# q and k stacked by way of DRAM, and probabilities turned by transposing transfers instead of by TensorE

## The chip, the cores and the metric

The kernel runs on one core of a Trainium2 chip. The metric is device time in microseconds, the median of several executions. The five engines (TensorE or PE, VectorE or DVE, ScalarE or ACT, GpSimd or POOL, and SyncE or SP, which here only issues DMA transfers) run their own streams of instructions and meet on semaphores.

## The reference

64 graphs of 128 nodes with 384 features pass two pre-norm residual blocks, an attention with 12 heads and a graph network of two layers:

```
h = relu(layernorm(x))
q, k, v = h Wq^T, h Wk^T, h Wv^T + bv            # 12 heads of 32
scores = q k^T / sqrt(384) + 2 adj                # per head
p = softmax(scores); rows whose scores are all 0 give 0
x = x + (p v) Wo^T + bo
h = relu(layernorm(x))
for l in 0, 1:
    u_left, u_right = h (h Wl^T)^T, h (h Wr^T)^T  # / sqrt(384)
    u = u_left on and above the diagonal of adj, u_right below it (adj transposed)
    e = exp(u) * adj;  h = relu(norm((e / sum(e)) (h W_lin^T + b)) * a + b)
x = x + h
```

Inputs and output are 32-bit. The kernel keeps that precision by splitting each matmul operand into a high and a low part and adding three products (hi hi, hi lo, lo hi).

## The kernel before, in words

Two graphs (256 token rows) form a group; there are 32 groups. All weights are loaded once, split into high and low part, and stay in SBUF. Each group passes through a list of steps, and each engine has its own written-out list (the table ORDER), in which every step comes with an offset in groups: an engine goes through its list once for each group, and runs step s for group g + offset. So attention of group g + 1 interleaves with the first graph layer of group g and the second layer of group g - 1. Nothing is scheduled at run time; an engine stops at the first step whose semaphores are not there yet, and all behind it on that engine waits too. The table BANK gives each job of TensorE one of the eight PSUM banks; a job must wait until the one before it in its bank was read out (`wait_bank`).

The steps by name, with the digit j for the graph (0 or 1) and c for a third of the heads (four heads, 512 columns):

- T1a, T1b: transposes of the normed input (xn1); QK0 to QK2: q and k for all heads, six blocks of 128 features by 256 tokens, two a job; V0, V1: v.
- q3, k3 on SP (`stack`, line 294): transfers that stack high and low parts of q and k along the partitions (3 x 32), so that one matmul of a depth of 96 forms all three products of a head. Each reads 32 partitions of qk, and each of the two steps has 12.
- Sjc on TensorE: the scores of four heads; on VectorE Sjc: adds 2 adj, writes prob and takes the row's minimum; xjc on ScalarE: the exponential.
- Pjc: TensorE turns the four squares of probabilities (line 417, with the identity), ScalarE evicts the high part into pT (line 482), VectorE the low part (line 599). PVj: 36 matmuls of pT against v. pT has room for one graph, so a graph's Pjc wait for the PV of the graph before.
- OTj, WOj: attention output, transposed and projected. T2a, T2b: the second norm, transposed. N0k, HL0j, U0, C0j: first graph layer; HTa, HTb, N1k, HL1j, U1, C1j: second one. AT: adj transposed.

TensorE does the 24 transposes of a group in four places: four behind N02, eight behind C11, four ahead of PV0 and eight behind it.

## Time and profile before

| what | value |
|---|---|
| median of 3 runs | 1622.85 us (1622.07 to 1628.5) |
| the profiled execution | 1625.41 us, of which span 1623.7 us |
| PE busy | 1550.8 us (96%), 13888 matmuls |
| DVE busy | 1146.9 us (71%) |
| ACT busy | 922.7 us (57%) |
| POOL busy | 457.1 us (28%) |
| chain that ended last | PE 87%, SP's queue 7% |
| DMA | 76.19 MB, mean 47 GB/s |
| mean granted TensorE clock | 0.98 |

The span runs from the first to the last instruction of one profiled execution. Busy time counts an engine's instructions; matmuls overlap, so the distance between two starts in the timeline says more of a matmul's price than its length. The chain is followed back from the last instruction to what released each step. A group of rows names line, engine, operation, output and inputs, and shapes.

### The profile page before, as it was taken

Reading aid. Unit: us, or ns where it says so; the run is one execution under the profiler, and the core shown is the slowest. Engines: PE = TensorE matmul, PEld = TensorE weight load, DVE = VectorE, ACT = ScalarE, POOL = GpSimd, SP = SyncE. Lnnn points to the kernel's source line nnn. Section 1 sums busy time; section 2 is a strip of 40 time slices with the busy share of each in tenths; the row PEclk is TensorE's granted clock in tenths of the full one; section 3 lists DMA queues with packets and bytes.
Section 4 is the critical chain, followed back from the end, with each engine's and each line's share of the span. In section 5 each row is a group of like instructions: output and inputs, shape, how many; then the busy total and the mean of one; then the engine's idle time right before and its main releaser. Section 6 shows DMA issues by size and latency. Waiting matters only on the chain.

```text
span 1623.7 us, 39352 instructions
## 1 busy us (share of the span) xinstructions
PE 1550.8 (96%) x13888; PEld 1524.4 (94%) x13888; DVE 1146.9 (71%) x4303; ACT 922.7 (57%) x2155; POOL 457.1 (28%) x928
## 2 busy tenths in 40 slices
PE   3699999999999999999999999999999999999984
PEld 3699999999999999999999999999999999999974
DVE  5567777777777677776767777767777776777643
ACT  4456655566665566665556656555666655665632
POOL 4113222333232223322233323222332323332222
PEclk8789999999999999999999999999999999999996
DMA  6101112211112211112221111221111222111100
GB/s 212 40 21 41 43 50 54 53 44 31 47 44 50 54 50 30 42 44 50 53 54 43 33 45 44 50 53 50 33 40 42 53 50 53 46 30 46 31 11 20
DMA packets 116769, 76.19 MB, mean 47 GB/s; under 512 B 14282, under 2 KB 116432, under 8 KB 116576
## 3 DMA queue, kind: packets, MB, share of 16 engines
q1 hardware_dynamic: 116128, 73.06, 17.6%
q8 instruction: 115, 1.88, 0.5%
q14 instruction: 78, 0.64, 0.1%
q0 software_dynamic: 448, 0.60, 0.1%
HBM read 23.28 MB, written 12.58 MB: 22 GB/s over the span
## 4 chain that ended last, share of the span: by engine, by line
PE 87%; SPq 7%; DVE 2%; issue 1%; ACT 1%; DMA 1%; POOL 1%; DVEq 0%; ACTq 0%; POOLq 0%
PE bank L341 70%; SPq L297 6%; PE bank L417 5%; PE bank L347 4%; PE bank L410 3%; PE bank L401 3%; PE bank L423 1%; DMA k<-qk 1%; PE bank L435 0%; ACT prob L506 0%; DVE qk L599 0%; ACT qk L482 0%; SPq L304 0%; DMA x_sb<-x 0%; DVE weights L575 0%
## 5 line engine op out<-in xcount | busy, mean ns | idle before, releaser
L341 PE MATMUL bank<-h,weights 128*128 128x256 f32 x3456 | 429.9, 282 | 5.8 <-DVE h L740 5.1
L341 PEld LDWEIGHTS bank<-h,weights 128*128 128x128 f32 x3456 | 412.0, 190 | 6.7 <-issue 5.7
L506 ACT ACTIVATE prob<-prob,rmin 128x128 f32<-128x128 f32 x768 | 237.2, 404 | 49.9 <-DVE rmin L657 49.9
L341 PE MATMUL bank<-weights,h 128*128 128x384 f32 x1152 | 223.5, 338 | 0.0
L341 PE MATMUL bank<-hA,weights 128*128 128x256 f32 x1728 | 218.5, 283 | 1.4 <-DVE hA L599 1.4
L599 DVE TENSOR_TENSOR n<-bank,n 128x512 fp32r<-128x512 f32 x192 | 129.4, 687 | 122.8 <-ACT n L482 122.7
L341 PEld LDWEIGHTS bank<-hA,weights 128*128 128x128 f32 x1728 | 211.7, 190 | 1.7 <-DVE hA L599 1.7
L341 PEld LDWEIGHTS bank<-weights,h 128*128 128x128 f32 x1152 | 194.1, 188 | 0.0
L482 ACT ACTIVATE n<-bank 128x512 fp32r<-128x512 f32 x192 | 111.9, 606 | 113.9 <-PE bank L341 113.9
L657 DVE CUSTOM_DVE_ANT_0 prob<-bank,adj_sb 128x128 f32<-128x128 f32 x768 | 175.0, 287 | 0.2 <-issue 0.2
L482 ACT ACTIVATE qk<-bank 128x512 f16<-128x512 f32 x96 | 57.2, 595 | 170.5 <-PE bank L341 170.5
L341 PE MATMUL bank<-n,h 128*128 128x256 f32 x1152 | 153.4, 287 | 0.0
L599 DVE TENSOR_TENSOR pT<-bank,pT 128x512 f16<-128x512 f32 x192 | 125.2, 680 | 27.8 <-ACT pT L482 27.5
L341 PEld LDWEIGHTS bank<-n,h 128*128 128x128 f32 x1152 | 141.7, 191 | 0.2 <-issue 0.2
L800 POOL TENSOR_SCALAR less_mean_gnn<-mv_gnn 128x2 f32<-128x2 f32 x64 | 14.2, 222 | 426.8 <-DVE mv_gnn L604 426.8
L341 PE MATMUL bank<-weights,hA 128*128 128x384 f32 x576 | 115.3, 344 | 2.9 <-DVEq L589 2.9
L341 PE MATMUL bank<-weights,oT 128*128 128x384 f32 x576 | 115.4, 344 | 1.4 <-DVE oT L599 1.4
L482 ACT ACTIVATE pT<-bank 128x512 f16<-128x512 f32 x192 | 111.6, 625 | 2.1 <-PE bank L410 1.7
L417 PE MATMUL bank<-ident,prob 128*128 128x128 f32 x768 | 107.7, 277 | 3.9 <-ACT prob L506 3.9
L787 POOL TENSOR_SCALAR less_mean_ln<-mv_ln 128x2 f32<-128x2 f32 x64 | 14.2, 222 | 325.3 <-DVE mv_ln L604 325.3
L341 PEld LDWEIGHTS bank<-weights,hA 128*128 128x128 f32 x576 | 101.1, 190 | 3.1 <-issue 3.1
L341 PEld LDWEIGHTS bank<-weights,oT 128*128 128x128 f32 x576 | 99.0, 189 | 1.6 <-DVE oT L599 1.6
(107 smaller groups left out, 2652.2 us busy)
## 6 DMA issues: line engine op xcount, KB each, us to landing
q<-qk SPq DMA_DIRECT2D x384, 48.0 KB, 1.9
k<-qk SPq DMA_DIRECT2D x384, 48.0 KB, 2.0
x_sb<-x SPq DMA_DIRECT2D x32, 384.0 KB, 3.5
out<-x SPq DMA_DIRECT2D x32, 384.0 KB, 2.5
adj_sb<-adj SPq DMA_DIRECT2D x32, 128.0 KB, 2.1
prob<-w SPq DMA_DIRECT2D x4, 576.0 KB, 6.3
x<-w SPq DMA_DIRECT2D x3, 576.0 KB, 4.4
pT<-w SPq DMA_DIRECT2D x3, 576.0 KB, 5.4
```

What stands on the lines that cost most here:

```text
L297: sp.dma_start(dst[D * r:D * r + D, a:NH:HC, :], qk[D * a:D * a + D, part, first:first + C, :]).then_inc(s, 16)
L341: mm = pe.matmul(out, lhsT, rhs, start=(n == 0), stop=(n == len(pairs) - 1))
L347: mm = pe.transpose(bank(job)[:, n * T + j * P:n * T + (j + 1) * P], src[:, j, c * P:(c + 1) * P], ident[:, :])
L401: mm = pe.matmul(bank(step)[:, a * P:(a + 1) * P], q3[:, h, j * P:(j + 1) * P], k3[:, h, j * P:(j + 1) * P], start=True, stop=True)
L410: mm = pe.matmul(bank(step)[:, h * DA:(h + 1) * DA], pT[:, a, h, :], v2[:, b, j, h, :], start=(h == 0 and n == 0), stop=(n == 2), skip_gro ...
L417: mm = pe.transpose(bank(step)[:, a * P:(a + 1) * P], prob[:, j, c * HC + a, :], ident[:, :])
L423: mm = pe.transpose(bank(step)[:, c * P:(c + 1) * P], o_sb[:, j, c * P:(c + 1) * P], ident[:, :])
L482: act.activation(out, src, ACT.Copy).then_inc(s_hi, 1)
L506: e = act.activation(prob[:, j, h, :], prob[:, j, h, :], ACT.Exp, bias=rmin[:, j, h:h + 1], scale=-1.0)
L599: dve.tensor_tensor(out, src, hi_part if hi_part.dtype == F16 else hi_part.bitcast(F32), ALU.subtract).then_inc(free(job), 1)
L657: r = dve.tensor_tensor_reduce(prob[:, j, h, :], bank(step)[:, a * P:(a + 1) * P], adj_sb[:, p, j, :], -2.0, 3.0e38, ALU.add, ALU.min, rmi ...
L787: pool.tensor_scalar(less_mean[k][:, :], mv[k][:, :, 0], -1.0, None, ALU.mult)
```

## The change

Three things change.

First, q and k. Instead of 24 transfers from SBUF to SBUF, each QK job is stored to a scratch tensor in DRAM (qs0, qs1, qs2: 256 KB each), and q3 and k3 read it back in three loads each (192 KB, rows of 1536 B). The order of the heads inside q3 and k3 changes with that.

Second, the probabilities. TensorE turns nothing. ScalarE (ph) copies the exponentials to a 16-bit high part in SBUF, VectorE (pl) subtracts to form the low part, and SP turns each 128x512 piece of each part into pT with a transposing transfer (pth, ptl): twelve a group. PVj waits for the transfers' semaphores. prob now holds one graph and not two, so the scores Sjc of the next graph wait for the low part of the one before. The new tile pp holds both parts.

Third, all five tables of ORDER and the table BANK are rewritten; T1a, T1b and QK0 move to the end of the pass of the group before (offset 2), and U0's last steps to offset 0.

```diff
@@ ORDER (one line of each table; BANK and the rest are rewritten in the same way)
 "SP": [
-        ("out", -2), ("q3", 1), ("ld_x", 2), ("k3", 1), ("ld_adj", 2)],
+        ("out", -2), ("qs0", 1), ("ld_adj", 1), ("qs1", 1), ("qs2", 1), ("ld_x", 2), ("q3", 1), ("k3", 1), ("pth00", 1),
...
@@ -163,10 +165,13 @@
         hA = sb("hA", [P, 2, C, T], F32R)
         qk = sb("qk", [P, 2, 2 * C, T], F16)
         xn1 = qk[:, :, :, :].rearrange("p s c t -> p (s c t)").bitcast(F32).rearrange("p (g h) -> p g h", g=2 * G)[:, 0:G, :]
+
+        qk_dram = nc.dram_tensor("qk_parts", [2, P, 2, 2 * C, T], F16).ap()
         q3 = sb("q3", [3 * D, NH, T], F16)
         k3 = sb("k3", [3 * D, NH, T], F16)
         v2 = sb("v2", [P, 2, G, NH, DA], F16)
-        prob = sb("prob", [P, G, NH, P])
+        prob = sb("prob", [P, NH, P])
+        pp = sb("prob_parts", [P, 2, NH, P], F16)
         pT = sb("pT", [P, 2, NH, P], F16)
         o_sb = sb("o_sb", [P, G, H])
         oT = sb("oT", [P, 2, C, P], F32R)
@@ -212,7 +217,10 @@
         s_xn2 = [sem(f"xn2_{j}") for j in range(G)]
         s_xbo = [sem(f"x_plus_bo{j}") for j in range(G)]
         s_q3, s_k3 = sem("q3_in"), sem("k3_in")
+        s_qs = [sem(f"qk_out{k}") for k in range(3)]
         s_exp = [[sem(f"exps{j}{c}") for c in range(C)] for j in range(G)]
+        s_part = [[sem(f"prob_{n}{c}") for c in range(C)] for n in ("hi", "lo")]
+        s_turned = [[sem(f"prob_turned_{n}{c}") for c in range(C)] for n in ("hi", "lo")]
         s_stats = {k: sem(f"stats_{k}") for k in ("ln1", "ln2")}
         s_aggr = {k: sem(f"aggr_{k}") for k in ("ln1", "ln2")}
         s_row0 = [sem(f"row0_{j}") for j in range(G)]
@@ -237,14 +245,14 @@
         LOADS = ((0, 0), (1, 1), (2, 2), (3, 3), (4, 0), (5, 1), (6, 2), (7, 3), (8, 0), (9, 1))
         STAGE_OF = dict(LOADS)
         SPLIT_AFTER = {
-            "ACT": {"": (0,), "xn1_1": (1,), "T1b": (2, 3), "QK0": (4, 5), "QK1": (6,), "V1": (7,), "QK2": (8,), "V0": (9,)},
-            "DVE": {"ln1_ag": (0,), "T1b": (1, 2), "QK0": (3, 4), "QK1": (5,), "QK2": (6, 7), "V1": (8,), "V0": (9,)}}
+            "ACT": {"": (0,), "xn1_1": (1,), "T1a": (2, 3), "QK0": (4, 5), "QK1": (6,), "QK2": (7,), "V0": (8,), "V1": (9,)},
+            "DVE": {"ln1_ag": (0,), "T1a": (1, 2), "QK0": (3, 4), "QK1": (5,), "QK2": (6, 7), "V0": (8,), "V1": (9,)}}
 
         def staged(m):
-            prob_flat = prob[:, :, :, :].rearrange("p g h q -> p (g h q)")
             flat = (x1[:, :, :, :].rearrange("p k g h -> p (k g h)")[:, 0:C * H],
                     pT[:, :, :, :].rearrange("p s h q -> p (s h q)").bitcast(F32)[:, 0:C * H],
-                    prob_flat[:, 0:C * H], prob_flat[:, NH * P:NH * P + C * H])[STAGE_OF[m]]
+                    prob[:, :, :].rearrange("p h q -> p (h q)")[:, 0:C * H],
+                    pp[:, :, :, :].rearrange("p s h q -> p (s h q)").bitcast(F32)[:, 0:C * H])[STAGE_OF[m]]
             return flat.rearrange("p (c o) -> p c o", c=C)
 
         def wait_load(eng, m):
@@ -279,7 +287,7 @@
             eng.wait_ge(s_hi, hi_turn[job, g])
 
         PARTS = [(HI, HI), (HI, LO), (LO, HI)]
-        STACKED = 16 * 3 * HC
+        STACKED = 16 * 3
 
         block = ctx.enter_context(nc.Block())
 
@@ -291,10 +299,10 @@
                         sp.wait_ge(s_wlo, m - 3)
                     sp.dma_start(staged(m), w_d[m].rearrange("(c p) o -> p c o", p=P)).then_inc(s_wload[STAGE_OF[m]], 16)
 
-            def stack(dst, s, first, parts):
-                for a in range(HC):
-                    for r, part in enumerate(parts):
-                        sp.dma_start(dst[D * r:D * r + D, a:NH:HC, :], qk[D * a:D * a + D, part, first:first + C, :]).then_inc(s, 16)
+            def stack(dst, s, which, parts, p):
+                for r, part in enumerate(parts):
+                    heads = qk_dram[p, :, part, which * C:which * C + C, :].rearrange("(a d) c t -> d a (c t)", d=D)
+                    sp.dma_start(dst[D * r:D * r + D, :, :].rearrange("d (a c) t -> d a (c t)", a=HC), heads).then_inc(s, 16)
 
             def run(step, g):
                 p, n = g % 2, g // 2
@@ -309,17 +317,35 @@
                     wait_filled(sp, "AT", g - 2)
                     ge(sp, s_mask[1], g - 1)
                     sp.dma_start(adj_sb[:, p, :, :], adj_d[g * G:(g + 1) * G, :, :].rearrange("g p h -> p g h")).then_inc(s_adjin[p], 16)
+                elif step[:2] == "qs":
+                    k = int(step[2])
+                    ge(sp, s_q3, STACKED * (g - 1))
+                    ge(sp, s_k3, STACKED * (g - 1))
+                    wait_drained(sp, f"QK{k}", g)
+                    sp.dma_start(qk_dram[p, :, :, 2 * k:2 * k + 2, :], qk[:, :, 2 * k:2 * k + 2, :]).then_inc(s_qs[k], 16)
                 elif step in ("q3", "k3"):
                     for j in range(G):
                         for c in range(C):
                             wait_filled(sp, f"S{j}{c}", g - 1)
-                    wait_drained(sp, "QK1", g)
+                    sp.wait_ge(s_qs[1], 16 * (g + 1))
                     if step == "q3":
-                        wait_drained(sp, "QK0", g)
-                        stack(q3, s_q3, 0, (HI, LO, HI))
+                        sp.wait_ge(s_qs[0], 16 * (g + 1))
+                        stack(q3, s_q3, 0, (HI, LO, HI), p)
                     else:
-                        wait_drained(sp, "QK2", g)
-                        stack(k3, s_k3, C, (HI, HI, LO))
+                        sp.wait_ge(s_qs[2], 16 * (g + 1))
+                        stack(k3, s_k3, 1, (HI, HI, LO), p)
+                elif step[:2] == "pt":
+
+                    part, j, c = "hl".index(step[2]), int(step[3]), int(step[4])
+                    hs = slice(c * HC, (c + 1) * HC)
+                    if g == 0:
+                        sp.wait_ge(s_wlo, NW)
+                    sp.wait_ge(s_part[part][c], G * g + j + 1)
+                    if j == 0:
+                        wait_filled(sp, "PV1", g - 1)
+                    else:
+                        wait_filled(sp, "PV0", g)
+                    sp.dma_start_transpose(pT[:, part, hs, :], pp[:, part, hs, :].rearrange("p h q -> p (h q)")).then_inc(s_turned[part][c], 16)
                 elif step == "out":
                     for j in range(G):
                         sp.wait_ge(s_y[j], g + 1)
@@ -397,24 +423,18 @@
                     pe.wait_ge(s_q3, STACKED * (g + 1))
                     pe.wait_ge(s_k3, STACKED * (g + 1))
                     for a in range(HC):
-                        h = c * HC + a
-                        mm = pe.matmul(bank(step)[:, a * P:(a + 1) * P], q3[:, h, j * P:(j + 1) * P], k3[:, h, j * P:(j + 1) * P], start=True, stop=True)
+                        mm = pe.matmul(bank(step)[:, a * P:(a + 1) * P], q3[:, a * C + c, j * P:(j + 1) * P], k3[:, a * C + c, j * P:(j + 1) * P], start=True, stop=True)
                     mm.then_inc(full(step), 1)
                 elif step[:2] == "PV":
                     j = int(step[2])
                     wait_drained(pe, f"V{j}", g)
-                    for c in range(C):
-                        wait_drained(pe, f"P{j}{c}", g)
+                    for part in (HI, LO):
+                        for c in range(C):
+                            pe.wait_ge(s_turned[part][c], 16 * (G * g + j + 1))
                     for h in range(NH):
                         for n, (a, b) in enumerate(PARTS):
                             mm = pe.matmul(bank(step)[:, h * DA:(h + 1) * DA], pT[:, a, h, :], v2[:, b, j, h, :],
                                            start=(h == 0 and n == 0), stop=(n == 2), skip_group_check=True)
-                    mm.then_inc(full(step), 1)
-                elif step[0] == "P":
-                    j, c = int(step[1]), int(step[2])
-                    pe.wait_ge(s_exp[j][c], g + 1)
-                    for a in range(HC):
-                        mm = pe.transpose(bank(step)[:, a * P:(a + 1) * P], prob[:, j, c * HC + a, :], ident[:, :])
                     mm.then_inc(full(step), 1)
                 elif step[:2] == "OT":
                     j = int(step[2])
@@ -486,8 +506,8 @@
                 if step[:4] == "xn1_":
                     j = int(step[4])
                     act.wait_ge(s_ln["ln1"], g + 1)
-                    ge(act, s_q3, STACKED * g)
-                    ge(act, s_k3, STACKED * g)
+                    for k in range(3):
+                        ge(act, s_qs[k], 16 * g)
                     act.activation(xn1[:, j, :], x_sb[:, p, j, :], ACT.Relu, bias=shift["ln1"][:, j:j + 1], scale=scale["ln1"][:, j:j + 1]).then_inc(s_xn1[j], 1)
                 elif step == "T1a":
                     hi(step, g, hA[:, HI, 0:2, :], 2 * T, "p (c t) -> p c t", c=2)
@@ -503,15 +523,14 @@
                     j, c = int(step[1]), int(step[2])
                     wait_drained(act, f"S{j}{c}", g)
                     for h in range(c * HC, (c + 1) * HC):
-                        e = act.activation(prob[:, j, h, :], prob[:, j, h, :], ACT.Exp, bias=rmin[:, j, h:h + 1], scale=-1.0)
+                        e = act.activation(prob[:, h, :], prob[:, h, :], ACT.Exp, bias=rmin[:, j, h:h + 1], scale=-1.0)
                     e.then_inc(s_exp[j][c], 1)
-                elif step[0] == "P":
-                    j, c = int(step[1]), int(step[2])
-                    if j == 0:
-                        wait_filled(act, "PV1", g - 1)
-                    else:
-                        wait_filled(act, "PV0", g)
-                    hi(step, g, pT[:, HI, c * HC:(c + 1) * HC, :], HC * P, "p (h q) -> p h q", h=HC)
+                elif step[:2] == "ph":
+                    j, c = int(step[2]), int(step[3])
+                    hs = slice(c * HC, (c + 1) * HC)
+                    act.wait_ge(s_exp[j][c], g + 1)
+                    ge(act, s_turned[HI][c], 16 * (G * g + j))
+                    act.activation(pp[:, HI, hs, :], prob[:, hs, :], ACT.Copy).then_inc(s_part[HI][c], 1)
                 elif step[:2] == "OT":
                     j = int(step[2])
                     hi(step, g, oT[:, HI, :, :], H, "p (c q) -> p c q", c=C)
@@ -650,11 +669,12 @@
                     dve.wait_ge(s_adjin[p], 16 * (n + 1))
                     if g == 0:
                         dve.wait_ge(s_wlo, 8)
+                    ge(dve, s_part[LO][c], G * g + j)
                     wait_filled(dve, step, g)
                     take_wait(3 + j * C + c)
                     for a in range(HC):
                         h = c * HC + a
-                        r = dve.tensor_tensor_reduce(prob[:, j, h, :], bank(step)[:, a * P:(a + 1) * P], adj_sb[:, p, j, :],
+                        r = dve.tensor_tensor_reduce(prob[:, h, :], bank(step)[:, a * P:(a + 1) * P], adj_sb[:, p, j, :],
                                                      -2.0, 3.0e38, ALU.add, ALU.min, rmin[:, j, h:h + 1])
                     r.then_inc(free(step), 1)
                 elif step[0] == "r":
@@ -681,10 +701,12 @@
                         dve.scalar_tensor_tensor(out=o_sb[:, j, :].rearrange("p (h d) -> p h d", h=NH), in0=pv[:, :, 0:D], scalar=-1.0,
                                                  in1=rinv[:, j, :].unsqueeze(2).to_broadcast([P, NH, D]),
                                                  op0=ALU.mult, op1=ALU.mult).then_inc(free(job), 1)
-                elif step[0] == "P":
-                    j, c = int(step[1]), int(step[2])
+                elif step[:2] == "pl":
+                    j, c = int(step[2]), int(step[3])
                     hs = slice(c * HC, (c + 1) * HC)
-                    lo(step, g, pT[:, LO, hs, :], pT[:, HI, hs, :], HC * P, "p (h q) -> p h q", h=HC)
+                    dve.wait_ge(s_part[HI][c], G * g + j + 1)
+                    ge(dve, s_turned[LO][c], 16 * (G * g + j))
+                    dve.tensor_tensor(pp[:, LO, hs, :], prob[:, hs, :], pp[:, HI, hs, :], ALU.subtract).then_inc(s_part[LO][c], 1)
                 elif step[:2] == "OT":
                     lo(step, g, oT[:, LO, :, :], oT[:, HI, :, :], H, "p (c q) -> p c q", c=C)
                 elif step[:2] == "WO":

```

Where the steps land. First TensorE from PV0 (36 matmuls of v and pT) to PV1, before: the transposes of prob stand on both sides of PV0, PV1 comes before QK0 (18 matmuls of hA and weights).

```order
L417 MATMUL bank<-ident,prob 128x128 x4
L410 MATMUL bank<-v,pT 128x33 x36
L417 MATMUL bank<-ident,prob 128x128 x8
L435 MATMUL bank<-ident,adj_sb 128x128 x2
L341 MATMUL bank<-n,h 128x256 x18
L423 MATMUL bank<-ident,o_sb 128x128 x3
L341 MATMUL bank<-weights,h 128x384 x9
L341 MATMUL bank<-bias_rows,pick 128x384
L347 MATMUL bank<-ident,qk 128x128 x6
L410 MATMUL bank<-v,pT 128x33 x36
```

The same place afterwards; S10 (k, q) is just ahead of PV0.

```order
L426 MATMUL bank<-k,q 128x128 x4
L436 MATMUL bank<-v,pT 128x33 x36
L367 MATMUL bank<-n,h 128x256 x18
L373 MATMUL bank<-ident,qk 128x128 x6
L367 MATMUL bank<-weights,h 128x384 x9
L367 MATMUL bank<-bias_rows,pick 128x384
L443 MATMUL bank<-ident,o_sb 128x128 x3
L367 MATMUL bank<-hA,weights 128x256 x18
L367 MATMUL bank<-weights,oT 128x384 x9
L367 MATMUL bank<-hl,dT 128x386 x6
L436 MATMUL bank<-v,pT 128x33 x36
```

No transposes of prob are left. Between the two PV jobs stand U0, T1, HL01, OT0, QK0, WO0, C00 and C01; QK0, WO0 and the C jobs were behind PV1 before.

Second, SP's queue over one group, before: q3, the load of x, k3, the load of adj, the result.

```order
L297 DMA q<-qk 32x3x256 x12
L304 DMA x_sb<-x 128x2x384
L297 DMA k<-qk 32x3x256 x12
L311 DMA adj_sb<-adj 128x2x128
L326 DMA out<-x 128x2x384
```

Afterwards:

```order
L352 DMA out<-x 128x2x384
L325 DMA qk_parts<-qk 256x1x512
L319 DMA adj_sb<-adj 128x2x128
L325 DMA qk_parts<-qk 256x1x512 x2
L312 DMA x_sb<-x 128x2x384
L305 DMA q<-qk_parts 32x4x768 x3
L305 DMA k<-qk_parts 32x4x768 x3
L348 DMA_TRANSPOSE pT<-prob_parts 128x4x128 x12
```

The 24 small transfers became three stores and six loads, and twelve transposes stand behind them, ahead of the next group's result and stores.

Third, TensorE behind QK2 up to the first scores, afterwards (before, the scores stood behind all of N1, HL10, T2, U1 and HL11):

```order
L367 MATMUL bank<-hA,weights 128x256 x18
L367 MATMUL bank<-weights,oT 128x384 x9
L373 MATMUL bank<-ident,c_sb 128x128 x6
L367 MATMUL bank<-weights,hA 128x384 x9
L367 MATMUL bank<-bias_rows,pick 128x384
L367 MATMUL bank<-weights,hA 128x384 x9
L367 MATMUL bank<-bias_rows,pick 128x384
L367 MATMUL bank<-h,weights 128x256 x36
L426 MATMUL bank<-k,q 128x128 x4
```

The first scores now come behind WO1, HT, V0, V1 and two N1 jobs, and the other scores are spread over the pass in fours.

## Rows read from the trace of the kernel before

**Rows 1.** Busy time by stretch: stretch, its length, each engine, clock, DMA share, GB/s.

```profile
core 0: us, PE busy (x) PEld busy (x) DVE busy (x) ACT busy (x) POOL busy (x), PEclk, DMA share, GB/s
200.00:400.00 200.00, 199.88 (x1834) 197.30 (x1832) 148.86 (x560) 116.26 (x275) 56.97 (x117) 1.00 0.18 46
4.00:6.00 2.00, 0.00 (x0) 0.00 (x0) 1.26 (x5) 0.25 (x1) 0.36 (x2) 1.00 1.07 403
```

**Rows 2.** TensorE in order of time: start us, length us, engine, line, what.

```profile
803.39 0.83 PE L401 MATMUL bank<-k,q 96*128 96x128 f16 x12
...
808.81 0.60 PE L417 MATMUL bank<-ident,prob 128*128 128x128 f32 x4
809.17 0.77 PE L341 MATMUL bank<-hl,dT 128*128 128x386 f32 x3
...
810.60 1.03 PE L417 MATMUL bank<-ident,prob 128*128 128x128 f32 x8
811.39 2.30 PE L341 MATMUL bank<-h,weights 128*128 128x256 f32 x18
...
815.27 0.60 PE L417 MATMUL bank<-ident,prob 128*128 128x128 f32 x4
815.70 1.06 PE L410 MATMUL bank<-v,pT 128*128 128x33 f16 x36
816.61 1.07 PE L417 MATMUL bank<-ident,prob 128*128 128x128 f32 x8
817.52 0.38 PE L435 MATMUL bank<-ident,adj_sb 128*128 128x128 f32 x2
...
851.25 0.83 PE L401 MATMUL bank<-k,q 96*128 96x128 f16 x12
...
1522.09 0.84 PE L401 MATMUL bank<-k,q 96*128 96x128 f16 x12
```

**Rows 3.** Groups by line: shapes, count, busy us, mean ns, idle before.

```profile
L506 ACT ACTIVATE prob<-prob,rmin 128x128 f32<-128x128 f32 x768 | 237.2, 404 | 49.9 <-DVE rmin L657 49.9
...
L599 DVE TENSOR_TENSOR pT<-bank,pT 128x512 f16<-128x512 f32 x192 | 125.2, 680 | 27.8 <-ACT pT L482 27.5 <-issue 0.2
...
L482 ACT ACTIVATE pT<-bank 128x512 f16<-128x512 f32 x192 | 111.6, 625 | 2.1 <-PE bank L410 1.7
L417 PE MATMUL bank<-ident,prob 128*128 128x128 f32 x768 | 107.7, 277 | 3.9 <-ACT prob L506 3.9
```

**Rows 4.** The queue of SP in order of time, one stretch.

```profile
832.50 7.69 SPq L297 DMA_DIRECT2D q<-qk  x12
```

**Rows 5.** Transfers: what, count, KB each, median us to landing.

```profile
k<-qk SPq DMA_DIRECT2D x384, 48.0 KB, 2.0
x_sb<-x SPq DMA_DIRECT2D x32, 384.0 KB, 3.5
out<-x SPq DMA_DIRECT2D x32, 384.0 KB, 2.5
adj_sb<-adj SPq DMA_DIRECT2D x32, 128.0 KB, 2.1
prob<-w SPq DMA_DIRECT2D x4, 576.0 KB, 6.3
```

**Rows 6.** TensorE in order of time, from U0 to C00.

```profile
817.66 2.40 PE L341 MATMUL bank<-n,h 128*128 128x256 f32 x18
...
822.62 1.06 PE L410 MATMUL bank<-v,pT 128*128 128x33 f16 x36
823.53 1.83 PE L341 MATMUL bank<-weights,oT 128*128 128x384 f32 x9
...
828.38 0.49 PE L423 MATMUL bank<-ident,o_sb 128*128 128x128 f32 x3
```

**Rows 7.** TensorE in order of time, behind QK2.

```profile
832.95 1.75 PE L341 MATMUL bank<-weights,oT 128*128 128x384 f32 x9
...
838.70 6.28 PE L341 MATMUL bank<-h,weights 128*128 128x256 f32 x54
844.82 1.73 PE L341 MATMUL bank<-weights,h 128*128 128x384 f32 x9
```

24 lines of the change are left out of this document (12 added, 12 removed), and 40 rows, old and new, of the table ORDER.

## The prediction, on record before the changed kernel ran

> **What bounds the kernel now.** I read the busy shares by stretch first. Between 200 and 400 us TensorE is busy 199.9 of 200 us at a granted clock of 1.00, VectorE 148.9, ScalarE 116.3, and the DMA engines 18% [rows 1]. So TensorE sets the pace, and nothing is lost to waits there. The timeline of TensorE gives the pace itself: the twelve score matmuls of a group start at 803.39, those of the next at 851.25, and fifteen groups later than the first at 1522.09. That is 47.86 us for one group and (1522.09 - 803.39) / 15 = 47.91 us in the mean [rows 2]. 32 groups of 47.9 us are 1533 us; the remaining 91 us of the span of 1623.7 us are start and end, where the pipeline fills and drains. What takes time out of TensorE's row is worth its full length, as long as every input still arrives in time. What only shortens VectorE or ScalarE is worth nothing.
>
> **What the change removes from TensorE.** The 24 transposes of the probabilities of each group. Their grouped row says 107.7 us busy for 768, 277 ns each [rows 3], but matmuls overlap, so the distance between starts is the better measure: 808.81 to 809.17 is 0.36 us for four, 810.60 to 811.39 is 0.79 for eight, 815.27 to 815.70 is 0.43 for four, 816.61 to 817.52 is 0.91 for eight [rows 2]. Together 2.49 us a group, 79.7 us for 32 groups. The busy time of 107.7 us is the upper end, 79.7 the value I take; the lower end is nothing, if a new wait stands in the gap. All other matmuls stay in number and shape, so the new pace is 47.9 - 2.5 = 45.4 us if TensorE stays full.
>
> **ScalarE and VectorE.** Six evictions of 128x512 from PSUM on each (625 ns and 680 ns [rows 3]) become six copies or subtractions of the same 512 columns out of SBUF. Neither output nor element count changes; I take no difference. Even 0.1 us more for each of twelve would be hidden: VectorE would have 149/200 x 47.9 = 35.7 us of work in 45.4. The exponentials stay.
>
> **SP's queue.** Before, 24 small transfers stack q and k: twelve take 7.69 us, 0.64 us each [rows 4], about 15.4 us a group. Afterwards there are 3 stores to DRAM, 6 loads, and 12 transposes. The trace has no transpose, so its two costs are bounded: the time h that it holds the queue, and the time L from issue to landing. For h the lower end is 0.64 us [rows 4]; the upper end is its whole landing. For L the nearest rows are 48 KB in 2.0 us, the lower end, and 128 KB in 2.1; upper ends are 384 KB in 3.5 and 576 KB in 6.3 [rows 5]. I take h = 1.2 us, twice a plain issue, because the transfer must be cut into many blocks, and L = 2.9, which is the 2.1 of 128 KB with that extra hold and a little for the turning. Both are estimates. The queue then has 12 x 1.2 + 9 x 0.64 + three others at about 0.5 = 21.7 us of work in 45.4. It is not full; but it is in order, and all depends on where it must deliver.
>
> **Tightest place: PV1.** pT has room for one graph. The six transposes of graph 1 wait until PV0 has read it, and PV1 waits for all six. Between them TensorE now has U0, T1, HL01, OT0, QK0, WO0, C00 and C01. Before, the same work ran from 817.66 to 828.38 with PV1 in its midst (822.62 to 823.53): 10.72 - 0.91 = 9.81 us [rows 6], less 0.15 us for the tail of PV0's last matmul: 9.65 us of cover. Needed are five holds and one landing: 5 x 1.2 + 2.9 = 8.9 us. At the bounds the need is 5 x 0.64 + 2.0 = 5.2 us, which costs nothing, and 6 x 6.3 = 37.8, which costs 28 us a group. The last data is no later: ph10 stands behind the evictions of T1 on ScalarE. U0 is 18 matmuls of 256 columns, as an N job is (2.0 us [rows 7]), T1 six transposes at 0.1 us; then come two evictions (0.9), ph10 (0.6) and on VectorE pl10 (0.7) [rows 3]: about 4.9 us behind PV0, before the sixth transpose's turn at 6.0. So PV1 finds its data with about 0.7 us to spare. PV0's own six have over 20 us of matmuls behind S01; I cost them at nothing.
>
> **Second place: S00.** Scores of the next group now stand after N12 and N10, not after HL11. Behind QK2, TensorE has WO1, HT, V0, V1 (832.95 to 838.70, 5.75 us) and two of three N jobs (6.12 x 2/3 = 4.08) [rows 7]: 9.8 us. Needed: eviction 0.6 + 0.7 with handovers, 1.5 us; then SP issues qs2, ld_x and three q3 loads (5 x 0.6 = 3.0; qs2 lands meanwhile in 2.5, as the 384 KB store [rows 5]), two k3 issues (1.3), and the third lands after 3 us (between 2.0 and 3.5): 8.8 us. Bandwidth: 384 + 1152 KB at the 403 GB/s of the first weight loads [rows 1] is 3.9 us, and fits between. About 1 us to spare.
>
> **The sum.** The profiled execution took 1625.4 us (span 1623.7 and 1.7 around it), 2.6 us above the median of 1622.85. 1625.4 - 79.7 = 1545.7 us; against the median 1543.2. With two margins under 1 us and all tables rewritten I add 0.25 us a group for short stalls, 8 us: **1551 us**. Start and end stay: the first groups have fewer issues for q and k, but a longer way from exponential to PV0.
>
> **Two rules of the Trainium skill on the transposing transfer.** Rows first: a plain 128 KB transfer lands in 2.1 us [rows 5]. "Advanced Engine Details and Errata", X-Bar Transpose, says that on this chip such a transfer is as fast as a plain one; by that, L is 2.1 to 2.5 and the sum stays at 1543 to 1551. "VectorE: DVE Perf Modes", The three transpose paths, gives 1309 ns for one 128x128 square in 2-byte numbers, against 390 ns on TensorE; with four squares in series that would be 5.2 us a transfer, an estimate from that page alone, and far above 2000 us for the kernel. No run here shows either; the second speaks against the change and stands beside the third rival.
>
> **Rivals.**
> 1. *q and k come late* (S00 waits). If six loads into 32 partitions each run below the rate of the weight loads, or land in 4.5 us, the need becomes 10.3 to 11 us against 9.8: about 1.2 us a group, 38 us, 1589 us. For it: only 1 us to spare, and ld_x goes ahead of them. Against: DMA is busy 18% of the time.
> 2. *The transposes are a little slow.* With 5h + L between 9.65 and 12.1 us PV1 waits for a part of the gain; in the middle 1.2 us a group, 1589 us again, by 12.1 us all is lost.
> 3. *Slower: each transpose holds the queue until it has landed* (h = L). Place: SP between PV0 and PV1. It decides from 5h + L = 9.65 + 2.49 = 12.1 us, h about 2.0. At 2.1 us (128 KB) the need is 12.6, 0.5 us a group above break-even: 1623 + 32 x 0.5 = 1639. At 2.8, midway to the 384 KB load, it is 16.8: 4.7 us a group lost, 1773. At 3.5 it is 21 us, 1908. For it: a chain of six with one buffer pays any hold six times. Against: plain transfers leave the queue after 0.64 of 2.0 us. The square rule above would fall here.
> 4. *The gap does not become time.* The single probability buffer (S1c waits for the subtraction of S0c) or the new bank table stalls TensorE 2.5 us a group: no change, 1623. Against: between S02 and S12, and between S01 and S11, stand two larger jobs of TensorE each, about 4 us, and four exponentials (404 ns each, overlapped [rows 3]), copy and subtraction need about 3.
>
> **Chances.** Forecast 0.55 (own range 1538 to 1570), first rival 0.15, second 0.12, third 0.14, fourth 0.04. A measurement of this kernel can tell 0.5%, some 8 us, from no change. Faster: 0.55 + 0.15 + 0.12 = 0.82; within 0.5%: 0.04; slower: 0.14. Eight in ten: the low end is 1538, a gain a little over 79.7 us (the whole 107.7 would give 1515, which counts overlapped time twice); the high end, reaching into the mild part of the third rival, 1640.
>
> **What would show it.** Right: distance between groups about 45.5 us, TensorE without a wait from 100 us on, no row of the transposes of prob on it, its wait for pT and k3 near nothing; SP's timeline with transposes 1.2 us apart and landing under 3.6. Wrong: TensorE's PV matmuls waiting for the DMA into pT, with transposes over 1.4 us apart (second or third rival); score matmuls waiting for k (first); waits for VectorE on a bank (fourth); or a granted clock under 1.00 in mid-kernel, as in the first 100 us, which would follow from such waits and make them dearer.

## The result and the profile after

The changed kernel takes 1643.15 us in the median of four runs (1639.69 to 1653.48); the kernel before took 1624.3 beside it. The ratio is 1.012, with a 95% interval from 1.0075 to 1.0165: slower by more than 0.5%, where 1551 us was forecast. The profiled execution took 1639.69 us.

The page of the changed kernel: busy time by engine, the chain that ended last, and its transfers with KB each and us to landing.

```profile
PE 1495.5 (91%) x13120; PEld 1459.9 (89%) x13120; DVE 1207.0 (74%) x4303; ACT 921.3 (56%) x2155; POOL 483.2 (30%) x928
...
PE 73%; DMA 13%; SPq 7%; issue 3%; DVE 3%; ACT 1%; POOL 1%; DVEq 0%; POOLq 0%; ACTq 0%
...
qk_parts<-qk SPq DMA_DIRECT2D x96, 256.0 KB, 2.5
q<-qk_parts SPq DMA_DIRECT2D x96, 192.0 KB, 4.5
k<-qk_parts SPq DMA_DIRECT2D x96, 192.0 KB, 5.5
x_sb<-x SPq DMA_DIRECT2D x32, 384.0 KB, 4.1
out<-x SPq DMA_DIRECT2D x32, 384.0 KB, 2.7
pT<-prob_parts SPq DMA_TRANSPOSE x384, 2.5
```

TensorE lost exactly the 768 transposes (13888 matmuls before, 13120 now) and about 55 us of busy time, where the forecast took 79.7 out. But transfers, 1% of the chain before, are 13% of it now. The landings answer to [rows 5]: the three loads of 192 KB into k3 take 5.5 us in the median, longer than 384 KB of x, and the transposing transfer takes 2.5.

Busy time by stretch, the answer to [rows 1]; the columns are the same.

```profile
200.00:400.00 200.00, 190.97 (x1683) 186.79 (x1682) 155.04 (x549) 116.39 (x275) 61.89 (x115) 0.99 0.42 93
...
844.00:846.00 2.00, 2.00 (x16) 2.00 (x15) 1.33 (x7) 0.18 (x1) 0.44 (x2) 1.00 0.82 252
846.00:848.00 2.00, 2.00 (x20) 2.00 (x19) 1.37 (x6) 0.43 (x1) 0.92 (x3) 1.00 0.97 274
848.00:850.00 2.00, 1.66 (x15) 1.45 (x13) 1.41 (x3) 2.00 (x5) 1.34 (x4) 1.00 0.91 188
```

TensorE is now idle for 9 us of 200, where it was idle for 0.1. From 846 to 850 us the DMA engines are nearly full (shares 0.97 and 0.91) and move only 274 and 188 GB/s; the first weight loads moved 403 [rows 1].

TensorE's waits: what waited for what, us in total, times, longest. In the changed kernel L426 is the line of the score matmuls, L436 that of PV, and L367 a helper that issues most of the others. "issue" names no engine: the profile shows nothing that TensorE waited for.

```profile
PE bank L426 <- DMA k<-qk_parts: 62.1, 31, 6.7
PE bank L367 <- issue: 13.9, 30, 3.1
PE bank L436 <- DMA pT<-prob_parts: 12.6, 5, 10.4
PE bank L367 <- DVEq L608: 11.1, 1, 11.1
```

The first scores wait for k in nearly every group. PV waits for pT five times, 10.4 of 12.6 us at the start. In order of time, on TensorE and then on SP's queue:

```profile
829.13 2.29 PE L367 MATMUL bank<-hA,weights 128*128 128x256 f32 x18 [0.35 <-issue]
...
837.27 2.37 PE L367 MATMUL bank<-hA,weights 128*128 128x256 f32 x18
839.47 1.75 PE L367 MATMUL bank<-weights,oT 128*128 128x384 f32 x9
...
851.23 0.38 PE L426 MATMUL bank<-k,q 96*128 96x128 f16 x4 [1.58 <-DMA k<-qk_parts]
```

```profile
839.34 2.26 SPq L325 DMA_DIRECT2D qk_parts<-qk  x2
841.99 0.38 SPq L312 DMA_DIRECT2D x_sb<-x  x1
842.66 1.71 SPq L305 DMA_DIRECT2D q<-qk_parts  x3
844.66 1.25 SPq L305 DMA_DIRECT2D k<-qk_parts  x3
```

QK2 starts at 837.27 and the job behind it at 839.47. The third load of k3 is issued at about 845.5, lands 5.6 us later, and TensorE goes on at 851.23. The distance of the first scores of two groups answers to [rows 2]: group 2 stands at 128.72 and group 31 at 1523.20, that is 48.09 us a group. Before, the same two stand at 133.04 and 1522.09, 47.90 us. So the middle of the program has won nothing.

### The profile page after: what moved, and what is told of

It is laid out like the page before. It is cut to its first block, busy times and chain, and to the rows that moved or that the text cites. A ratio compares the mean times of both kernels' runs of the same rounds, so it can differ in the third digit from the quotient of the medians.

```text
span 1638.0 us, 38385 instructions
## 1 busy us (share of the span) xinstructions
PE 1495.5 (91%) x13120; PEld 1459.9 (89%) x13120; DVE 1207.0 (74%) x4303; ACT 921.3 (56%) x2155; POOL 483.2 (30%) x928
## 4 chain that ended last, share of the span: by engine, by line
PE 73%; DMA 13%; SPq 7%; issue 3%; DVE 3%; ACT 1%; POOL 1%; DVEq 0%; POOLq 0%; ACTq 0%
PE bank L367 62%; DMA k<-qk_parts 11%; SPq L305 4%; PE bank L436 4%; PE bank L426 3%; PE bank L373 3%; SPq L348 1%; PE bank L443 1%; DVE x L717 1%; SPq L312 1%; DMA pT<-prob_parts 1%; DMA qk_parts<-qk 1%; DMA pT<-w 0%; PE bank L455 0%; DMA x_sb<-x 0%
## 5 line engine op out<-in xcount | busy, mean ns | idle before, releaser
L367 PE MATMUL bank<-h,weights 128*128 128x256 f32 x3456 | 435.9, 284 | 5.7 <-DVE h L762 4.7
L367 PEld LDWEIGHTS bank<-h,weights 128*128 128x128 f32 x3456 | 418.1, 192 | 6.7 <-issue 6.7
L526 ACT ACTIVATE prob<-prob,rmin 128x128 f32<-128x128 f32 x768 | 244.3, 394 | 23.1 <-DVE rmin L677 22.9
L367 PE MATMUL bank<-hA,weights 128*128 128x256 f32 x1728 | 229.8, 287 | 11.8 <-issue 9.8
L367 PE MATMUL bank<-weights,h 128*128 128x384 f32 x1152 | 229.9, 344 | 0.0
L367 PEld LDWEIGHTS bank<-hA,weights 128*128 128x128 f32 x1728 | 212.9, 191 | 18.8 <-issue 16.8
L367 PEld LDWEIGHTS bank<-weights,h 128*128 128x128 f32 x1152 | 197.2, 190 | 0.0
L842 POOL TENSOR_TENSOR x_sb<-x_sb,bo_all 128x384 f32<-128x384 f32 x64 | 65.0, 1016 | 442.9 <-ACT qk L511 437.6
L709 DVE TENSOR_TENSOR prob_parts<-prob,prob_parts 128x512 f16<-128x512 f32 x192 | 151.9, 791 | 7.1 <-ACT prob_parts L533 6.9
L367 PE MATMUL bank<-n,h 128*128 128x256 f32 x1152 | 153.1, 287 | 0.3 <-DVE n L618 0.3
L367 PEld LDWEIGHTS bank<-n,h 128*128 128x128 f32 x1152 | 141.4, 191 | 0.7 <-issue 0.7
L502 ACT ACTIVATE oT<-bank 128x384 fp32r<-128x384 f32 x64 | 31.5, 492 | 192.7 <-PE bank L443 192.7
L426 PE MATMUL bank<-k,q 96*128 96x128 f16 x768 | 76.2, 225 | 62.1 <-DMA k<-qk_parts 62.1
L367 PE MATMUL bank<-weights,hA 128*128 128x384 f32 x576 | 117.2, 348 | 11.1 <-DVEq L608 11.1
L533 ACT ACTIVATE prob_parts<-prob 128x512 f16<-128x512 f32 x192 | 120.2, 626 | 2.7 <-DMA pT<-prob_parts 1.5
L426 PEld LDWEIGHTS bank<-k,q 96*128 96x128 f16 x768 | 50.9, 100 | 75.8 <-issue 72.6
L367 PE MATMUL bank<-weights,oT 128*128 128x384 f32 x576 | 114.6, 344 | 3.2 <-DVE oT L618 3.2
L367 PEld LDWEIGHTS bank<-weights,hA 128*128 128x128 f32 x576 | 103.1, 192 | 11.3 <-issue 11.3
```

What stands on the lines that cost most here:

```text
L367: mm = pe.matmul(out, lhsT, rhs, start=(n == 0), stop=(n == len(pairs) - 1))
L426: mm = pe.matmul(bank(step)[:, a * P:(a + 1) * P], q3[:, a * C + c, j * P:(j + 1) * P], k3[:, a * C + c, j * P:(j + 1) * P], start=True, s ...
L502: act.activation(out, src, ACT.Copy).then_inc(s_hi, 1)
L526: e = act.activation(prob[:, h, :], prob[:, h, :], ACT.Exp, bias=rmin[:, j, h:h + 1], scale=-1.0)
L533: act.activation(pp[:, HI, hs, :], prob[:, hs, :], ACT.Copy).then_inc(s_part[HI][c], 1)
L709: dve.tensor_tensor(pp[:, LO, hs, :], prob[:, hs, :], pp[:, HI, hs, :], ALU.subtract).then_inc(s_part[LO][c], 1)
```

## The experiments

Theory A: the 2.5 us a group that the transposes took are free now, and the wait for k, with what follows from it, eats them. Its rivals name other holders: the DRAM route as such, the latency of one load and not its bytes, the transposing transfers, slow VectorE operations. Distances below are means from group 2 to 31 unless said otherwise; medians are in us, with the ratio to the kernel before and its interval. Of the waits for k, 9 to 12 us stand in the first two groups in each version of the changed kernel in this table.

| kernel | median | ratio | wait of TensorE for k (times) | k lands in |
|---|---|---|---|---|
| changed kernel | 1643.15 | 1.012 (1.0075 to 1.0165) | 62.1 (31) | 5.5 |
| S00 behind N11 | 1588.44 | 0.9771 (0.9754 to 0.9789) | 13.3 (6) | 5.4 |
| third loads cut | 1601.92 | 0.9849 (0.9829 to 0.9869) | 28.2 (27) | 4.4, the cut one 4.6 |
| x behind k | 1600.25 | 0.985 (0.9836 to 0.9865) | 23.0 (21) | 4.5 |
| loads to 128 partitions | 1587.78 | 0.9768 (0.9751 to 0.9784) | 19.1 (17) | 3.7 |
| before, DRAM route alone | 1617.57 | 0.9944 (0.9927 to 0.9961) | 15.9 (2) | 5.4 |
| before, transposing transfers alone | 1706.8 | 1.0503 (1.0482 to 1.0525) | 71.5 (32) | 1.9 |

**The first scores one job later.**

```diff
 "PE":
-  ("N10", -1), ("S00", 1), ("N11", -1), ("T2b", 0), ...
+  ("N10", -1), ("N11", -1), ("S00", 1), ("T2b", 0), ...
 (on VectorE S00 goes behind N11 too)
```

> The changed kernel with one move: S00 stands behind N11 instead of ahead of it, on TensorE and VectorE (one N job, 2.05 us, more cover for the loads of q3 and k3). Theory A (the scores wait for k3 because 1.5 MB of loads move at only some 225 GB/s, a wait of 1.75 us in each of 30 groups, and it alone eats the gain): the wait for k all but goes, the distance between groups falls from 47.9 to about 46.0 us, the time from 1643 to 1580-1592 us. Theory B (the re-sequencing as a whole is too tight, and another wait takes the place): distance stays above 47.3 us, time 1625-1643 us, with a new wait for a bank or for pT on TensorE.

Measured: 1588.44 us. k still lands in 5.4 us, but TensorE now has one more job of about 2.1 us ahead of S00. 49 of the 62 us of waiting are gone, and 55 us of time. The distance of first scores is 46.44 us. From group 2 on, TensorE waits for k only four times, 2.0 us in all. Theory A holds: it was the place of this one step that made the changed kernel slower than the kernel before. The 37 us that are left above the forecast of 1551 it does not explain.

**The DRAM route alone, in the kernel before.**

```diff
 "SP": [
-  ("out", -2), ("q3", 1), ("ld_x", 2), ("k3", 1), ("ld_adj", 2)],
+  ("out", -2), ("qs0", 1), ("qs1", 1), ("qs2", 1), ("q3", 1), ("ld_x", 2), ("k3", 1), ("ld_adj", 2)],
```

> The kernel before with the q and k route alone: three stores to DRAM and six loads a group instead of 24 small transfers; order of all compute engines as before, TensorE still turns the probabilities. Theory A (the route is harmless where the first scores come late, since here they stand behind N11, HL10, T2, U1 and HL11, 8.5 us later): no wait for k in mid-kernel, distance 47.9 us, time within 0.5% of before, 1616-1630 us. Theory C (the way through DRAM costs time by itself, in contention or latency): over 1635 us with waits for k in the middle.

Measured: 1617.57 us, a little faster than before. k lands in 5.4 us here too, and apart from two waits at the start nobody waits for it: S00 stands behind HL11 in that order. The same slow load costs nothing in one order and 55 us in another. The small gain has its place too, the even pace: the kernel before waits for k in five groups of the middle, 2.3 us in all, and its first scores are 47.90 us apart; here they are 47.72 to 47.73 apart in every group.

**Bytes or latency.** The third load of each of q3 and k3 is cut to an eighth.

```diff
-  sp.dma_start(dst[D * r:D * r + D, :, :]..., heads)
+  n = C * T // 8 if r == 2 and g > 0 else C * T
+  sp.dma_start(dst[D * r:D * r + D, :, :]...[:, :, 0:n], heads[:, :, 0:n])
```

> The changed kernel; from the second group on the third load of q3 and of k3 brings only an eighth of its bytes (the rest of those rows stays from the first group, so the low-high product of the scores is left out in part). Issues, waits and order are the same; 344 KB less in each burst. Theory A (the wait is bytes over a rate of some 225 GB/s): k3 lands 1.5 us earlier, the wait falls from 1.75 to 0.2-0.4 us, time about 1590-1602 us. Theory D (the wait is latency of store, load and issue, whatever the bytes): landing of k3 stays over 5 us, time 1636-1645 us.

Measured: 1601.92 us. The full loads of k land in 4.4 us, and the third, with 24 KB, in 4.6; it stands behind the others in the queue. With as many loads and fewer bytes, the wait falls by more than half. A fixed latency would have left it.

**The place of x.** ld_x goes behind k3.

```diff
-  ("qs2", 1), ("ld_x", 2), ("q3", 1), ("k3", 1), ("pth00", 1),
+  ("qs2", 1), ("q3", 1), ("k3", 1), ("ld_x", 2), ("pth00", 1),
```

> The changed kernel with one transfer moved on SP: the load of x (384 KB) goes out behind the six loads of q3 and k3 instead of ahead of them, and the first norm's statistics stand later on VectorE to match; TensorE's order is untouched. If the bytes ahead of k3's last load at its rate decide when k lands (the theory), 384 KB less at some 225 GB/s is 1.7 us earlier, TensorE's wait for k (62.1 us) falls below 15 us, and 1590 to 1605 us come out, with x landing later and nobody waiting for it. Rival: only the bytes to 32 partitions count, which the load of x (128 partitions) does not share; then k lands less than 0.7 us earlier and the time stays above 1620 us.

Measured: 1600.25 us; k in 4.5 us, x in 5.3. k lands 1 us earlier, less than the 1.7 expected but more than the rival's 0.7. The wait left is 23.0 us, above the 15 expected. The short wait ahead of QK0, 0.35 us a group in the changed kernel, grows to about 0.5 and has a name here: 18.1 us in 30 times for the low part of hA on VectorE. Bytes to all partitions count too, as bytes ahead in the same queue.

**Where the loads go.** The same 192 KB in the same 1536 B rows, but to 128 partitions.

```diff
+  if g > 0:
+      rows = qk_dram[p, :, part, which * C:which * C + C, :].rearrange("p c t -> p (c t)")
+      sp.dma_start(dst[:, 4 * r:4 * r + 3, :].rearrange("p h t -> p (h t)"), rows)
```

> The changed kernel with its order untouched; from the second group on the six loads that fill q3 and k3 bring the same 192 KB each, in the same rows of 1536 B, but spread over 128 partitions instead of 32, so the scores are computed from wrongly placed data. Theory P (the loads are slow because each goes to 32 partitions only, which takes about half of the rate: some 225 GB/s at a full DMA share against 403 GB/s of the first weight loads): k lands 3.5 to 4 us after issue instead of 5.5, TensorE's wait at the first scores for k goes almost wholly (62.1 us to under 15), 1580 to 1595 us. Theory Q (reading DRAM in rows of 1536 B, or the number of bytes at that moment, sets the rate): k lands at 5.5 us as before, wait and time as the changed kernel's, about 1640 us.

Measured: 1587.78 us; q in 3.6 us and k in 3.7, against 4.5 and 5.5. Two windows of this kernel, behind its k3 issue, which begins at 820.15:

```profile
822.00:824.00 2.00, 2.00 (x19) 2.00 (x18) 1.20 (x6) 0.95 (x3) 1.61 (x6) 1.00 1.02 363
824.00:826.00 2.00, 1.76 (x18) 1.59 (x17) 0.92 (x4) 1.76 (x4) 0.15 (x1) 1.00 0.11 39
```

At a full share, 363 GB/s flow where 188 to 274 flowed before, and the burst ends by about 824.2. The bytes and the size of the rows are the same, so neither sets the rate; the narrow destination does (besides it, only the order in which the rows are read changes). The wait (19.1 us) is a few us above the 15 expected: 10.4 us stand in the first two groups, and single later ones still miss by 0.2 to 1.2 us. Groups that do not wait for k are 45.75 to 46.26 us apart.

The Trainium skill, "SBUF — State Buffer", Door 1: The DMA port swizzle, says that partitions 0 to 31, and 0 to 63 as well, reach only half of the 16 ports of SBUF, and that 128 partitions reach all. The trace agrees in direction, and roughly in size: 188 to 274 GB/s near a full share, against 363 and 403. That it is the ports, and not merely the count of partitions, no run here separates; the three loads of each step go to partitions 0 to 31, 32 to 63 and 64 to 95.

**The transposing transfers alone.** The kernel before, with probabilities split in SBUF and turned by transfer, and the old 24 small transfers for q and k; its order and banks are written anew.

> The kernel before with one part of the change: the probabilities are split in SBUF and turned by 12 transposing transfers a group; q3 and k3 are filled by the old 24 small transfers from SBUF. Order and banks are written anew for this mix. If the removed transposes are what pays (the theory), TensorE's work per group is about 45.5 us instead of 48.0, and 1590 to 1615 us come out as long as k is in time; the trace must show no row of TensorE that turns prob and few waits for k. Rival: 24 small transfers and 12 transposing ones on one queue make k or pT late, TensorE waits over 1.5 us a group for a DMA, and the time is 1625 to 1660 us.

Measured: 1706.8 us, slower even than the rival's range. Its SP queue in one group, and four waits of TensorE:

```profile
799.61 18.29 SPq L343 DMA_TRANSPOSE pT<-prob_parts  x12
...
826.55 7.67 SPq L306 DMA_DIRECT2D q<-qk  x12
834.32 0.54 SPq L313 DMA_DIRECT2D x_sb<-x  x1
835.15 8.59 SPq L306 DMA_DIRECT2D k<-qk  x12
```

```profile
PE bank L421 <- DMA k<-qk: 71.5, 32, 9.8
PE bank L431 <- DMA pT<-prob_parts: 26.5, 24, 8.6
PE bank L362 <- DVE n L613: 18.2, 28, 1.4
PE bank L362 <- DVE dT L743: 12.3, 15, 2.9
```

Each transfer of k lands in 1.9 us, but the last one is issued 17 us after the first of q. The queue is busy for about 36 us a group: 18 us of transposes in a row, then 17 us of stacking in a row. This speaks for keeping the two parts of the change together, since the DRAM route needs nine issues (three stores, six loads) where the old one needs 24. It is not shown: the order of this kernel is its own, so the 5% are not the price of the transfers alone.

**Both parts in two new orders.** All tables are rewritten; the core on TensorE of the second of them:

```diff
-  ("V0", 1), ("V1", 1), ("N12", -1), ("N10", -1), ("S00", 1), ("N11", -1), ("T2b", 0), ("HL10", -1), ...
+  ("V1", 1), ("V0", 1), ("N10", -1), ("T2b", 0), ("T2a", 0), ("N11", -1), ("N12", -1), ("HL10", -1), ("S00", 1), ...
```

> Both parts of the change with all order tables and the banks written once more: the first scores stand behind the last N1 job and further behind k's loads, the second graph's transposing transfers open SP's pass, and the two preparations at the start are fewer. If waits alone separate the changed kernel from its TensorE work (45.5 us a group), this comes out at 1560 to 1580 us, under the 1588 us of the version with only the first scores moved, with TensorE's wait for k under 10 us. Rival: the pace is set by something shared (slow subtractions, a clock that drops), then it stays at 1588 us or above.

> A second such writing of order and banks for both parts, which differs in where the steps of the second graph layer stand. Expected within 10 us of the one beside it, 1560 to 1585 us, if TensorE's work and not a certain order sets the time; 1590 us or above if single waits decide.

Measured: 1638.12 us (ratio 1.0074, 1.0047 to 1.01) and 1585.74 us (0.9751, 0.9726 to 0.9776). I expected 1560 to 1580 and 1560 to 1585 us, within 10 us of each other. The second is just above that, and the first is 52 us behind it, so single waits decide. The first lost its gain to two other waits; these are TensorE's in it, and then the longest in the second:

```profile
PE bank L372 <- DVE oT L623: 44.6, 31, 2.6
PE bank L441 <- DMA pT<-prob_parts: 31.4, 31, 3.0
```

```profile
PE bank L372 <- issue: 23.8, 31, 0.8
```

The second has no wait for k beyond the start (13.6 us in 2). Its 23.8 us come from one place, the first matmuls on dT. The high and low part of dT stand on VectorE behind the sum y0, which took 1.37 us there beside a GpSimd addition that ran from 801.00 to 802.08 (y1, beside nothing, took 0.55):

```profile
801.13 1.37 DVE L757 SCALAR_TENSOR_TENSOR x<-c_sb,x 128x384 f32<-128x384 f32 x1
```

**y0 moved.**

```diff
 "DVE":
-  ... ("U0.d", 0), ("y0", -1)]  and at the start  ("U0.dh", -1), ("U0.dl", -1), ("HL01", -1), ("y1", -2)
+  ... ("U0.d", 0)]              and at the start  ("U0.dh", -1), ("U0.dl", -1), ("HL01", -1), ("y0", -2), ("y1", -2)
```

> The fastest version so far (1585.74 us) with one step of VectorE moved: the sum that closes the second graph layer for the first graph (y0) stood between U0's product and U0's last steps, took 1.37 us there beside GpSimd (0.55 us beside nothing), and TensorE then waited 0.78 us for dT; now y0 goes behind HL01. If the wait is a matter of order, its 23.8 us in 31 go mostly (under 10 left), and 1562 to 1575 us come out. If another step beside GpSimd takes the delay over, the time stays at 1580 us or above.

Measured: 1576.82 us (0.9703, 0.9688 to 0.9717), the fastest complete version: 3% under the kernel before and 4% under the changed one. The wait falls to 9.7 us in 31. That is just inside the expectation; the time is 1.8 us above it. First scores are 46.12 us apart.

**GpSimd beside VectorE.** In the version with S00 behind N11, za and zb work on 8 columns of 384 and leave out the others.

```diff
-  pool.tensor_tensor(c_sb[:, j, :], c_sb[:, j, :], lna_all[:, :], ALU.mult)
+  pool.tensor_tensor(c_sb[:, j, 0:8], c_sb[:, j, 0:8], lna_all[:, 0:8], ALU.mult)
 (zb likewise)
```

> The version with the first scores behind N11 (1588.44 us), whose four GpSimd steps za and zb a group work on 8 of their 384 columns; scale and bias of the last norm are left out on the other columns. Theory C (VectorE's operations out of SBUF slow down while GpSimd works in SBUF): the subtraction of the probabilities falls from a mean of 794 ns to under 720, the product by adjT (791 ns) likewise, and the wait of 0.34 us ahead of QK0 in 30 groups gets shorter by half or more; 1572 to 1583 us. Rival: the slow subtractions come from the transfers that read and write SBUF at that time; then the means stay above 770 ns and the time within 3 us of 1588 us.

Measured: 1575.18 us (0.9688, 0.967 to 0.9706), 13 us under the same kernel with full work on GpSimd. The subtraction of the probabilities and the product by adjT on VectorE, first with full, then with light GpSimd:

```profile
L714 DVE TENSOR_TENSOR prob_parts<-prob,prob_parts 128x512 f16<-128x512 f32 x192 | 152.4, 794 | 8.1 <-ACT prob_parts L538 6.0 <-DMA pT<-prob_parts 1.0
...
L747 DVE TENSOR_TENSOR work<-work,adjT 128x256 f32<-128x256 f32 x64 | 50.6, 791 | 0.5 <-ACT work L563 0.5
```

```profile
L714 DVE TENSOR_TENSOR prob_parts<-prob,prob_parts 128x512 f16<-128x512 f32 x192 | 138.1, 719 | 8.0 <-ACT prob_parts L538 6.9
L747 DVE TENSOR_TENSOR work<-work,adjT 128x256 f32<-128x256 f32 x64 | 39.7, 621 | 0.5 <-ACT work L563 0.5
```

Both fall, and the row of 30 waits of 0.34 us ahead of QK0 is gone from TensorE's list. Theory C of this expectation holds: while GpSimd runs such an operation on SBUF, VectorE's operations with two inputs in SBUF stretch. The first scores are 46.15 us apart in the mean, against 46.44 with full work on GpSimd; most groups stand at 45.6 to 46.2, and only one comes down to the 45.4 of the forecast.

**The same work on VectorE.** za and zb go from GpSimd to VectorE in the version with y0 moved, and y1 goes behind PV1.

```diff
 "DVE":
-  ("HL01", -1), ("y0", -2), ("y1", -2), ("QK0", 1), ... ("PV1.o", 0), ("OT1", 0),
+  ("HL01", -1), ("za0", -2), ("zb0", -2), ("y0", -2), ("QK0", 1), ... ("PV1.o", 0), ("za1", -2), ("zb1", -2), ("y1", -2), ("OT1", 0),
```

> The version with y0 moved (1576.82 us) with the four steps za and zb a group (scale and bias of the last norm, 128x384 in SBUF, 1.1 us each on GpSimd) taken over by VectorE, which needs some 0.55 us for such an operation; y1 goes behind the second graph's attention output. Theory C (GpSimd's work in SBUF slows VectorE's): the subtraction of the probabilities falls from 873 ns to under 740, the wait of 0.30 us for dT in 31 groups shrinks or goes, the distance of first scores falls from 46.1 to about 45.7 us, and 1560 to 1572 us come out. Rival: the 2.2 us more a group on VectorE delay an attention output that TensorE waits for, and the time stays at 1575 us or above.

Measured: 1656.62 us (1.0206, 1.0185 to 1.0227), 85 us above the top of the expectation. SP's queue, TensorE, and VectorE in this kernel:

```profile
841.72 0.40 SPq L357 DMA_DIRECT2D out<-x  x1
```

```profile
845.14 1.85 PE L372 MATMUL bank<-weights,oT 128*128 128x384 f32 x9 [2.29 <-DVE x L722]
```

```profile
829.00 1.37 DVE L714 TENSOR_TENSOR prob_parts<-prob,prob_parts 128x512 f16<-128x512 f32 x1
...
832.30 0.67 DVE L714 TENSOR_TENSOR prob_parts<-prob,prob_parts 128x512 f16<-128x512 f32 x1
...
844.53 0.56 DVE L722 TENSOR_TENSOR x<-bank,x_sb 128x384 f32<-128x384 f32 x1 [2.42 <-issue]
...
L722 DVE TENSOR_TENSOR x<-bank,x_sb 128x384 f32<-128x384 f32 x64 | 35.7, 558 | 106.7 <-issue 45.0 <-PE bank L372 34.9 <-DMA out<-x 26.9
```

The rival had the range and an output that comes late, but not the way there. The transfer of the result waits for y1. The sum that writes x for the group two later (L722) needs the same buffer, so it must wait until that transfer has read it: issue at 841.72 and 2.7 us of landing give 844.4. TensorE then waits for the bank of WO0, 66.4 us in 30 times, and the first scores are 48.99 us apart. The subtraction fell only from 873 to 810 ns, where less than 740 was expected. The long one above coincides with GpSimd's other SBUF operation, x plus bo, which ran from 828.80 to 829.82; the next, beside nothing, took 0.67 us. The product by adjT came down from 584 to 416 ns.

## Why the prediction was wrong

The failed step is "Second place: S00", in its last term: "the third lands after 3 us (between 2.0 and 3.5)", backed by "384 + 1152 KB at the 403 GB/s of the first weight loads [rows 1] is 3.9 us, and fits between". The chain up to the issue was right. It said 1.5 + 3.0 + 1.3 = 5.8 us from QK2 to the last issue; the job behind QK2 starts at 839.47, and about 845.5 is 6.0 later. The landing was 5.6 us there, and 5.5 in the median of all loads of k, outside the bounds given. The need is 11.76 us (839.47 to 851.23) where 8.8 was forecast and 9.8 was covered. The bounds came from loads of 48 KB, which do go to 32 partitions, but only one every 0.64 us [rows 4], some 77 GB/s, and from one load of 384 KB to 128 partitions. The trace of before has no burst of large loads to 32 partitions, and the rate was taken from a load of another shape. So the first rival is what happened; its place and cause were named, and its need of 10.3 to 11 us was still 0.8 short.

Its price was too small as well: at 1589 us it still stood under the kernel before. Against the profiled execution, 1545.7 us without any stall, the new one took 94 us more:

- The middle, from the first scores of group 2 to those of group 31: 29 x (48.09 - 45.4) = 78 us. Of it, 49 are the wait for k (62.1 us less 4.5, 6.7 and 1.9 for groups 0 to 2).
- About 10 us of the 78 are the wait ahead of QK0, 0.35 us in each group. The prediction took no difference on VectorE. The subtraction out of SBUF has a mean of 791 ns, where the eviction had 680 [rows 3], and the experiment with light GpSimd shows the cause. The 8 us added for short stalls were meant for such things and did not cover them.
- In the remaining 19 us of the 78 TensorE does not wait, it is busy for longer (1333.4 us in this stretch, where 1386.4 before less 72.2 for the transposes would be 1314.2). About 5 of them are the clock. Three times the granted clock falls to near the lower of its two levels for 3 to 4 us: behind the wait for k of 2.54 us at 272.56 (rows below), behind one of 1.81 at 610.64 (0.57 over 612 to 616) and behind one of 1.89 at 1331.26 (0.57 over 1332 to 1336). One minus the clock, times the length, is 1.7 us each time. The N job there takes 3.07, 3.15 and 3.50 us instead of 2.30. Behind the longest wait of the middle, 2.67 us at 1381.59, it did not fall, and the kernel before has no such place in its middle. About 5 more, an estimate, are lost overlap: QK2 and the job behind it overlap by 0.17 us (837.27 + 2.37 against 839.47), and each of the 28 waits for k takes that away. Some 9 us, 0.3 a group, are not settled; the 45.4 may have been a little low.

```profile
272.56 0.38 PE L426 MATMUL bank<-k,q 96*128 96x128 f16 x4 [2.54 <-DMA k<-qk_parts]
272.75 3.07 PE L367 MATMUL bank<-h,weights 128*128 128x256 f32 x18
...
851.43 2.30 PE L367 MATMUL bank<-h,weights 128*128 128x256 f32 x18
```

```profile
272.00:276.00 4.00, 3.44 (x25) 3.47 (x25) 1.58 (x10) 0.14 (x1) 0.00 (x0) 0.77 0.00 0
276.00:280.00 4.00, 4.00 (x27) 3.95 (x26) 1.54 (x8) 2.76 (x9) 0.00 (x0) 0.81 0.02 4
```

- "Start and end stay" failed. By its place in the order (some 8.5 us of work earlier, from the third N job, 842.8 by [rows 7], to 851.25 in [rows 2]) and two groups without transposes (5.0), S00 of group 2 should have come 13.5 us earlier; it comes 4.3 earlier (128.72 against 133.04), so 9.2 us are lost. At the start PV0 waits 10.4 us for the first pT and V0 11.1 for constants (2.9 before), and the granted clock up to these scores is 0.81, against 0.86 before. From the first scores of the last group to the end it was 101.6 us; with 8.5 more for S00's place and 2.5 less for the transposes 107.6 were due, and it is 114.8: 7.2 us lost. No experiment was made on the start or the end. 78 + 9.2 + 7.2 is the 94.

What was right: the 24 transposes do turn into time once little waits. The first scores are 46.12 us apart in the fastest complete version, against 47.90 before: 1.8 us a group. The full 2.5 was reached by one group only, in the version with light GpSimd. The transposing transfer holds the queue for 1.2 us (median 1216 ns of 384) and lands in 2.5, where h = 1.2 and L = 2.9 were taken; that h came out so well was luck, as no row of before showed it. PV1 waits for hardly anything in mid-kernel, so the second and third rival fell. The fourth fell: no wait for prob or a bank. The rule of the Trainium skill, "Advanced Engine Details and Errata", X-Bar Transpose, which the prediction weighed, says that such a transfer is as fast as a plain one. The landing agrees, 2.5 us beside the 2.1 of a plain 128 KB [rows 5]; the time that the queue is held does not, 1.2 us beside about 0.6. The figure of 1309 ns a square in the Trainium skill, "VectorE: DVE Perf Modes", The three transpose paths, does not add up over four squares, since the whole piece lands in 2.5 us.
